# A four-layer graph network on one Trainium2 core: the edge term of the last two layers' finishing moved from GpSimd to the tensor engine

## The reference, cut to what matters

```
def _transformer_conv(x, src, dst, ea, Wq, bq, Wk, bk, Wv, bv, We, Ws, bs, H, C):
    q, k, v = (x @ Wq + bq), (x @ Wk + bk), (x @ Wv + bv)      # (n, H, C), 4 heads of 32
    e = (ea @ We).reshape(-1, H, C)                            # ea: one weight for each edge
    alpha = einsum('ehc,ehc->eh', q[dst], k[src] + e) / sqrt(C)
    p = exp(alpha - segment_max(alpha, dst)[dst])
    w = p / segment_sum(p, dst)[dst]
    out = segment_sum((v[src] + e) * w[..., None], dst)
    return out + x @ Ws + bs
...
h = _transformer_conv(h, ...1)
out = _transformer_conv(h, ...2)
return x + out
```

## Time and profile before

| | us |
|---|---|
| time before, median of 3 runs (lowest, highest) | 3722.99 (3717.47, 3732.42) |
| the profiled execution's own time | 3726.67 |
| its span, first to last instruction | 3724.8 |
| mean granted tensor clock over the span | 0.702 |
| PE busy / DVE busy / ACT busy / POOL busy | 2389.6 / 1711.9 / 1147.3 / 2460.8 |
| first edge-attention layer's finishing, from done_mark to the next layer's first gather | 3061.26 to 3109.55 |
| second one's finishing, from done_mark to the last output row | 3686.25 to 3721.59 |

### The profile page before, as it was taken

How to read it: one execution, slowest core, us unless ns; L and a number is a source line. 1 busy time by engine, 2 the same in 40 slices (tenths; PEclk the granted TensorE clock), 3 DMA queues, 4 the chain that set the end, 5 groups by cost and what they waited for, 6 DMA issues and landing times.

```text
span 3724.8 us, 44708 instructions
## 1 busy us (share of the span) xinstructions
PE 2389.6 (64%) x12460; PEld 1788.2 (48%) x12460; DVE 1711.9 (46%) x3957; ACT 1147.3 (31%) x2849; POOL 2460.8 (66%) x2561
## 2 busy tenths in 40 slices
PE   3498888755445554554454544456787885788777
PEld 2476666333333433333343333335666664666665
DVE  4365555432232332222232222235777664666777
ACT  2366655400000110000000000035666642666662
POOL 1777775077777457777667777627777735777773
PEclk9988778955555555555555555567989987889897
DMA  4543332312222111212122222146666626666661
GB/s 94 87 85 85 84 78 48 141 51 53 53 53 53 36 52 53 53 52 53 45 59 53 53 52 53 43 123 186 182 180 180 180 64 174 180 181 183 180 181 34
DMA packets 345058, 356.74 MB, mean 96 GB/s; under 512 B 125614, under 2 KB 267637, under 8 KB 344821
## 3 DMA queue, kind: packets, MB, share of 16 engines
q0 software_dynamic: 93184, 219.12, 22.4%
q1 hardware_dynamic: 245494, 132.86, 13.6%
q10 hardware_dynamic: 6148, 1.93, 0.3%
HBM read 323.81 MB, written 30.05 MB: 95 GB/s over the span
## 4 chain that ended last, share of the span: by engine, by line
POOL 57%; issue 19%; PE 13%; DVE 5%; DMA 3%; ACT 1%; ACTq 1%; SPq 1%; DVEq 0%; POOLq 0%
POOL gathered_rows L479 32%; POOL gathered_rows L465 25%; PE QX L1176 6%; PE NU L1176 3%; PE MTB L1176 3%; DMA gathered_rows<-key_value_rows,src_index 2%; DVE messages L732 1%; ACTq L531 1%; DMA query_window<-gat_target_scores 0%; PE MID L1176 0%; DMA open_tiles<-end_ahead_penalty 0%; DVE query_key_products L732 0%; DVE x_rows L732 0%; PE MID L1209 0%; PE MTB L1209 0%
## 5 line engine op out<-in xcount | busy, mean ns | idle before, releaser
L1176 PE MATMUL NU<-gathered_rows 128*128 128x128 f32 x2496 | 635.9, 436 | 787.1 <-DMA gathered_rows<-gcn_rows,src_index 524.5
L1176 PEld LDWEIGHTS NU<-gathered_rows 128*128 128x128 f32 x2496 | 553.6, 327 | 992.2 <-issue 973.9
L465 POOL DMA_INDIRECT gathered_rows<-key_value_rows,src_index x832 | 816.6, 982 | 318.3 <-issue 252.8
L479 POOL DMA_INDIRECT gathered_rows<-gcn_rows,src_index x832 | 786.7, 946 | 346.6 <-issue 253.0
L732 DVE TENSOR_TENSOR sums_transposed<-sums_transposed,NU 128x512 f32 x624 | 426.6, 684 | 1237.2 <-PE NU L1176 1236.2
L465 POOL DMA_INDIRECT gathered_rows<-gat_rows,src_index x416 | 403.9, 971 | 209.4 <-issue 124.7
L479 POOL DMA_INDIRECT gathered_rows<-relation_rows,src_relation_index x416 | 393.8, 947 | 148.1 <-issue 126.5
L659 ACT ACTIVATE edge_node_onehot<-iota_window,dst_in_window_by_edge 128x128 f32<-128x128 f32 x1248 | 394.6, 386 | 27.3 <-PE MTB L1176 25.1
L1176 PEld LDWEIGHTS NU<-edge_node_onehot,messages 128*128 128x128 f32 x2496 | 384.2, 220 | 16.9
L1176 PE MATMUL NU<-edge_node_onehot,messages 128*128 128x128 f32 x2496 | 384.0, 305 | 0.0
L1176 PE MATMUL MTB<-edge_node_onehot,edge_factors 128*8 128x128 f32 (+1 forms) x2496 | 358.7, 292 | 0.0
(11 more groups left out here) (257 smaller groups left out, 2579.3 us busy)
## 6 DMA issues: line engine op xcount, KB each, us to landing
query_window<-query_rows SPq DMA_DIRECT2D x832, 66.0 KB
dst_in_window_row<-dst_in_window SPq DMA_DIRECT2D x156, 256.0 KB
gathered_rows<-gcn_rows,src_index POOLq DMA_INDIRECT x832, 2.5
gathered_rows<-key_value_rows,src_index POOLq DMA_INDIRECT x832
relation_rows<-gathered_rows SPq DMA_DIRECT2D x25, 512.0 KB, 2.6
gathered_rows<-gat_rows,src_index POOLq DMA_INDIRECT x416
query_window<-gat_target_scores SPq DMA_DIRECT2D x416, 2.0 KB
gathered_rows<-relation_rows,src_relation_index POOLq DMA_INDIRECT x416, 2.5
```

The costliest lines, as they stand in the source:

```text
L465: pool.indirect_dma_start(out=rows_of(a, s)[:, t, :], out_offset=None, in_=a["table"], in_offset=bass.IndirectOffsetOnAxis(ap=srcI[:, TPG ...
L479: pool.indirect_dma_start(out=lrows[:, TPG * (K % LRING) + t, :], out_offset=None, in_=p["table"], in_offset=bass.IndirectOffsetOnAxis(ap= ...
L1176: return pe.matmul(o, l, r, start=start, stop=stop)
```

## The change

The edge term is no longer made on GpSimd. In `finish_block` of the two edge-attention layers the transpose of the sums becomes a matmul with the identity that leaves its accumulation open, and a second matmul adds, on the same PSUM tile, the 8 rows of extra sums times an 8 by 128 matrix WeT, whose rows 4 to 7 hold We of each head and whose rows 0 to 3 are zero. The multiplication by 1/S comes after both. The bias row is added by the vector engine in the first layer, straight from `brow`; for the second layer GpSimd adds the bias row once to all 25 blocks of xN, in one instruction behind the first edge-attention layer's gathers, and the vector engine adds xN. WeT is made at the start by two transposes and two copies; the two loads of WeB go. Since the extra sums are now read by every block, GpSimd clears extS only after the last block's matmuls.

```diff
-        WeB = [sb(f"edge_weight_row_{i}", [P, D]) for i in range(2)]
+        WeT = [sb(f"edge_weight_by_head_turned_{i}", [8, D]) for i in range(2)]
...
-        NWEIGHTS = 6 + 2 * 11 + 4 + 6
+        NWEIGHTS = 6 + 2 * 10 + 4 + 6
...
-            def edge_parts(j):
-
-                pool.wait_ge(S["part_ready"], j + 1)
-                for b0, b1 in ((0, 1), (1, 3), (3, 6), (6, 10), (10, 15), (15, 20), (20, NBK)):
...
-                    last.then_inc(S["edge_ready"], m)
...
             attention_gathers(4, ATT[1])
-            edge_parts(0)
-            pool.wait_ge(S["ext_psum"], 2)
+            pool.wait_ge(S["h_row"], 4 * NBK)
+            pool.tensor_tensor(xN[:, 0:NBK, :], xN[:, 0:NBK, :], brow[:, 2, :].unsqueeze(1).broadcast_to([P, NBK, D]), ALU.add
+                               ).then_inc(S["bias_added"], 1)
+            pool.wait_ge(S["fin_psum"], 4 * NBK)
             pool.memset(extS[:, 0:NV], 0.0).then_inc(S["ext_zeroed"], 1)
-            pool.wait_ge(S["fin_psum"], 4 * NBK)
             pool.memset(numS[:, 0:NV], 0.0).then_inc(S["zeroed"], 1)
             attention_gathers(5, ATT[2])
-            edge_parts(1)
...
-                load(WeB[q][:], A[f"L3_gnn_We{q + 1}"].broadcast_to([P, D]))
...
+                act.copy(WeT[q][:], QXf[0][0:8, 768 + D * q:768 + D * (q + 1)])
...
                 dve.wait_ge(S["fin_psum"], (3 + j) * NBK + b + 1)
-                if b == 0 or b in (1, 3, 6, 10, 15, 20):
-                    dve.wait_ge(S["edge_ready"], j * NBK + next(e for e in (1, 3, 6, 10, 15, 20, NBK) if e > b))
+                if b == 0 and j == 1:
+                    dve.wait_ge(S["bias_added"], 1)
...
-                tt(tmpB[:, b % 4, :], QXf[b % 2][:, 512:512 + D], edge_part[:, b, :], ALU.add).then_inc(S["fin_used"], 1)
+                tt(tmpB[:, b % 4, :], QXf[b % 2][:, 512:512 + D], xN[:, b, :] if j else brow[:, 1, :], ALU.add).then_inc(S["fin_used"], 1)
...
                 then(dve.reciprocal(exN2[:, 0:NBK, 4:8], exN2[:, 0:NBK, 0:4]))
-                tt(exN2[:, 0:NBK, 0:4], exN[:, 0:NBK, 4:8], exN2[:, 0:NBK, 4:8], ALU.mult).then_inc(S["part_ready"], 1)
...
             for q in range(2):
+                pe.transpose(QXf[0][0:8, 768 + D * q:768 + D * (q + 1)], WeH8[q][:], I[:])
                 mm(QXf[0][:, 512 + 4 * q:516 + 4 * q], wqT[:, q, :], WeH8[q][:, 4:8])
...
+                elif f > 2:
+                    mm(o, numT[:, w], I[:], stop=False)
+                    mm(o, extT[0:8, w], WeT[f - 3][:], start=False)
+                    last = mm(QXf[b % 2][:, 512:512 + D], hT[:, w], Wsk[f - 3][:])
                 else:
                     last = pe.transpose(o, hT[:, w] if f == 2 else numT[:, w], I[:])
-                    if f > 2:
-                        last = mm(QXf[b % 2][:, 512:512 + D], hT[:, w], Wsk[f - 3][:])
```

More of the change, by code:

```diff
@@ L197, in gnn_stack_kernel @@
         Sl = stage.rearrange("p (g t j) -> p g t j", t=TPG, j=P)
-        edge_part = ring[:, at_part:at_part + NV].rearrange("p (b d) -> p b d", d=D)
         squares = ring[:, at_part:at_part + N]
@@ L232, in gnn_stack_kernel @@
         QXf = [q[:].rearrange("p t w -> p (t w)") for q in QX]
-        names = """query_pads_stored tstored0 tstored1 tstored2 tstored3 tstored4 staged_odd part_ready ext_zeroed edge_ready
+        names = """query_pads_stored tstored0 tstored1 tstored2 tstored3 tstored4 staged_odd ext_zeroed bias_added
             spans_ready offsets_ready offsets_read consts_ready edges_zeroed edges_loaded dst_copied pads_stored dst_loaded x_zeroed x_loaded
```

## The result

The changed kernel takes 3769.73 us (median of 4 runs, 3765.61 to 3773.92), the one before 3726.34 beside it (4 runs, 3717.47 to 3732.42). The ratio on record is 1.0133, with an interval of 1.0117 to 1.0149; the two medians alone give 1.0116. It is slower by 1.2 to 1.3%, where no measurable difference was forecast (3712.2, range 3701 to 3728).

The account below looks back on a forecast made before the run. GpSimd's row gathers, untouched by the change, were taken as the bound. Terms -1.0 + 3.8 - 1.2 - 12.4 = -10.8 on the profiled 3726.67 gave 3715.9; less 3.7 to the runs' median, 3712.2 us, range 3701 to 3728.

Parts of the forecast that it names:

- Start: At the kernel's start, two weight loads fewer in a queue the vector engine waits for: -1.0 us.
- Tail: Behind the first edge-attention layer's gathers, GpSimd's long bias add holds the vector engine's messages sum: +3.8 us.
- Price of the new matmuls: In both finishings, three more passes per block cost 0.32 us, or 0.64 at the low clock.
- The clock: In the second finishing, the tensor engine works without a gap: three blocks at 1.28 us, then twenty at 0.72.
- First finishing: After the first edge-attention layer, an earlier start and no GpSimd adds outweigh slower last blocks: -1.2 us.
- The slow rival: First finishing, blocks 5 to 24: tensor engine bound at the low clock, +28 us there, 3752.6 in all; chance 0.03.
- Second finishing: After the second edge-attention layer, block 0 starts earlier and blocks mostly take 0.72 us: -12.4 us.
- The first rival: Second finishing: the clock does not come back, -1.2 us there, 3723.4 in all; chance 0.21.
- 21 us after 1/S: End of the second finishing: the last output row would come 21 us after the reciprocals in the changed profile.
- Clearings: End of the first finishing: GpSimd's two clearings after the last matmul fit into idle time, cost 0; otherwise 2.8 us.
- A1: Theory from the experiments on the finishings: time the tensor engine spends in passes of few rows keeps the clock low.

Follow-up runs that it names:

- the move alone: The changed kernel with the bias row added to xN ahead of the first edge-attention layer's gathers: 4607.67 us on the slower chip.
- the 64-row trace: The changed kernel with the edge product padded from 8 to 64 rows with zeros: 3735.2 us, one run.
- the grouped kernel: The changed kernel with its second finishing in groups of four blocks, a quarter of the changes of height: 3748.48 us, one run.
- the 8 by 8 product: The changed kernel with a 128-row edge product, plus an unread product of 8 rows over 8 columns per block: 4584.27 us on the slower chip.
- its control: The changed kernel with a 128-row edge product, plus an unread product of 128 rows over 8 columns per block: 4566.31 us on the slower chip.
- the 8 by 128 product: The changed kernel with a 128-row edge product, plus an unread product of 8 rows over 128 columns per block: 3773.8 us, one run.
- the 128-row version: The changed kernel with the edge product padded from 8 to 128 rows with zeros: 3698.06 us, 0.9951 of the kernel before.
- the 96-row one: The changed kernel with the edge product padded from 8 to 96 rows with zeros: 4555.59 us on the slower chip, one run.

## Why the prediction was wrong

By its own steps:

- **Start**, -1.0: the first gather of layer 1 starts at 91.17, 1.09 earlier than the 92.26 before. That fits, but it is not shown: in the seven experiments on chips of this speed, which leave out the same two loads, it starts at 91.75 to 92.95.
- **Tail**, +3.8: the add took 6.93 us (6.98 forecast), stretched a sum to 3.67 in place of 0.68, and the tail is 3.4 longer; the move alone shows 3.7 on the other chip. The mechanism is right. The size is less sure than these two numbers look: on the chips of about 3720 us the tail takes 44.0 to 47.9 us in the six traces with the add behind the gathers (mean 46.3) and 42.1 to 44.5 in the three without it (43.4). The Trainium skill's rule in "SBUF — State Buffer", section "Who interferes with whom", a hold for the whole instruction, agrees with this trace at 6.93 us as with that of before at 1.54. It spoke for this part of the forecast, and not against it as the prediction says.
- **Price of the new matmuls**, 0.32 us for three passes more: this is the first of the two steps that failed. It went by the columns, "as 128 columns are what the other passes share", and by the earlier trace rows, where 25 small transposes of 8 rows follow each other without a change between them. Three passes more and two changes of height are 0.74 at the full clock (1.06 - 0.32) and 1.23 (1.87 - 0.64) at the low one.
- **The clock**, taken as back at 1.00 for most of both finishings, in the second because the engine would "have work without a gap": the second step that failed, and the dearer one in the first finishing (some 31 us of clock to some 11 of changes, from the 64-row trace). The work has no gap in the busy column, 34.00 of 34.00, and the clock stayed at 0.50. The Trainium skill, "TensorE: Matmul & The Clock Gate", section "Part 1: The HAM clock gate (the "warmup" mystery)", says that the clock is set by how busy the engine has been. Read by the busy column the trace doesn't agree, but that column counts the time of a change as busy (39.62 of 40 us in the second finishing, where the passes alone are 1.28 of each 1.87), so it is no test of that rule. That the changes do it is shown for the second finishing, by the grouped kernel and the 8 by 8 product with its control; that it works through the idle time inside them is my reading, and no run shows it.
- **First finishing**, -1.2: +40.7. The slow rival had its place and kind right (turn, six passes and table at the low clock, 2.8 us for each block, +28) with a chance of 0.03; the 0.59 for the changes make it 3.38. Its condition was read from the earlier trace rows, where more work looked like more clock. Without the change of height this part of the forecast holds: 1.44 us a block for 1.45, and 46.5 in all for 48.3 before, -1.8.
- **Second finishing**, -12.4: +12.7. The first rival, the low clock throughout with a chance of 0.21, came true there, but it had no changes in it and gave -1.2; the 13.9 beyond that are the changes at the low clock (25 times 0.59 is 14.8). With 128 rows it is 25.6 against 38.6, -13.0: the whole of the forecast, blocks 0.76 for 0.72, is there as soon as the change of height is not. The "21 us after 1/S" of its last paragraph doesn't fit its own sum, which gives 19.7 (3709.2 - 3689.5); with 128 rows it is 19.1.
- **Clearings**, 0: both fitted, 5.5 us and then 4.47 idle. Right.

The sum of the four places as measured, -1.1 + 3.4 + 40.7 + 12.7, is +55.7; the traces differ by +39.0 and the medians by +43.4. The rest, -16.7 in the traces, is outside all of the change's places, and what made it is open.

Open: what holds the clock down in the first finishing, where most of the loss lies. With the 64-row edge product it was low for 10.3 us there, with the 8 by 8 product for 10.2, with the 8 by 128 product for 23.9, and with the 8-row edge product, in all three traces (89.0, 90.3, 90.4 us), at least until the edge products were over. All of them have two changes for each block, so the changes alone don't settle it there. The order is one that A1 would give, since the share of the time in 8-row passes grows along it, but each of the first three is one run, and none was made to separate A1 from A2 in this stage. What is shown for it is that an edge product of 8 rows keeps the clock low and one of 128 or 96 doesn't.

## What to carry to other kernels

Price a small matmul by its neighbours, not by its columns: between 128-row products one of 64 or of 8 rows cost two changes (about 0.4 us at the full clock), and with one such product for each block of short products the clock stayed at half, which cost more than the changes did. Pad the contraction to the neighbours' height with zero rows, or group the small products; both gave the clock back (the grouping was tried in the second finishing alone). And when a column says 100% busy at half clock, look at whether the weight loads run ahead of their matmuls.

## What the runs showed of the hardware that I had not expected

- In the second finishing a matmul over 96 rows behaves as one over 128 (25.6 us, 0.76 a block), one over 64 as one over 8 (51.3 both). In the first one 64 rows were much faster than 8 (57.8 against 89.0).
- One product of 8 by 8 for each block turned a stretch of 28.9 us into one of 57.2.
- The profile counts the change of height as busy time: 39.62 of 40.00 us in the second finishing, where the changes are 0.59 of each 1.87.
- The kernel before took about 3720 us on all chips but one, and 4566 on that one. The finishings agree within 2 us all the same: the changed kernel's (89.0 and 51.3) with those of its version with the bias row moved (90.4 and 53.1, on the slower chip), and the 128-row version's (46.5 and 25.6) with those of the 96-row one (48.1 and 25.6, on the slower chip).
